# First layer's middle batches: the older batch's routing moved behind the fourth turn and the second product, and two weight steps moved to GpSimd

## Chip, cores and metric

One NeuronCore of a Trainium2 chip runs the whole kernel. The metric is the device time in microseconds of one execution. Engine names: PE is TensorE, DVE VectorE, ACT ScalarE, POOL GpSimd, SP SyncE.

## What is computed

Two rounds of gated cross-attention and feed-forward on `x` of shape (4, 512, 256), with a context of 64 rows. Cut to what the change touches:

```python
x = x + tanh(g_xattn[0]) * xattn0(layernorm(x), ctx)    # 16 heads, then relu(out @ W1 + b1) @ W2 + b2
x = x + tanh(g_ffn[0]) * moe(layernorm(x))              # router: logits = layernorm(x) @ router_w + router_b
x = x + tanh(g_xattn[1]) * xattn1(layernorm(x), ctx)
x = x + tanh(g_ffn[1]) * bitlinear_mlp(layernorm(x))    # weights rounded to -1, 0, 1 times mean(abs(w))
```

The change lies in the first line's stage. Beside the attention of the first layer, that stage does two side jobs: the router's logits of each finished batch (the second line's `layernorm(x) @ router_w`), and the rounding of the three weight matrices of the fourth line.

## The kernel before, in words

The order on each engine is written out by hand: each engine has its own program, an endless sequence of instructions in program order, and waits on semaphores. Nothing is reordered. The function `attention(l, b, first_batch, last_batch)` exists once for each of PE, ACT and DVE, and `batch(l, b, first, last)` is the same stretch on POOL. `l` is the layer, `b` the batch (0 to 3). Batches 1 and 2 of layer 0 are the middle batches.

A batch has four tiles of 128 rows (`i` = 0 to 3). The work of a tile:

- `scores` on PE writes s_tile[i % 2] in PSUM. DVE takes the maximum (`score_max`, L1515) and subtracts it into `probs` (`score_sub`, L1524), ACT takes the exponential (`exps`, L1163), DVE sums and inverts (`sums`, L1537 and L1540), POOL multiplies by the inverse (`normalise`, L523).
- `turn(i)` on PE transposes the tile (L761) into `t_bank`, and ACT copies it out (`turned`, L1201). `values(half)` on PE multiplies two tiles with the values (L779), ACT rounds the result to `o_hi` (L1206), DVE makes the rest `o_lo` (`lower_outputs`, L1608).
- At the end of a batch PE does the first product (L831, 36 matmuls) and the second product (L846, 48 matmuls). ACT makes `h_t` and `h_hi` between them, DVE `h_lo` (L1613). DVE adds the result to `x_res` (L1679), and takes its statistics (L1453, L1462).

Tiles 0 and 1 of batch b+1 are scored, summed and normalised within batch b. So a batch opens with `turn(0)`, `scores(b, 2)`, `turn(1)`, `scores(b, 3)` on PE.

The routing of the older batch b-1: POOL computes `rstd` (`layer_norm_rstd`, L407 and L409), DVE writes the normalised rows to `xn2` (`norm_apply`, L1475: four instructions of 128x256, shown as `ew<-x_res,mv,rstd` because `xn2` lies in the memory of `ew2`), SP stores them, PE transposes them (`router_turn`, L901), ACT copies them to `xn_t` (`router_rows`, L1168), PE multiplies (`router_products`, L908), DVE adds the bias (`router_logits`, L1581).

The weight rounding of matrix w has three elementwise steps on 128x2048: `ternary_first` (L1571) and `ternary_second` (L1577) on DVE, `ternary` (L489) on POOL. In the last batch PE transposes the results in six chunks (`ternary_chunk`, L894) and ACT copies them. Chunks 4 and 5 are of matrix 2.

The second use of L1475 (`xn<-x_res,mv,rstd`) is the normalisation of the rows for batch b+2, in batches 0 and 1.

## Time and profile before

| | |
|---|---|
| median of 3 runs | 578.87 us (573.36 to 580.24) |
| profiled execution, its own time | 582.83 us |
| its span | 580.0 us, so 2.8 us lie around it |
| mean granted TensorE clock | 0.933 |
| stage of the change, layer 0's four batches | 30.0 to about 166 us of the span |
| batch 1 (67.4 to 102.8): busy us of PE, DVE, ACT, POOL | 31.9, 32.4, 18.0, 15.2 of 35.4 |
| batch 2 (102.8 to 136.9): the same | 31.9, 28.2, 18.1, 14.9 of 34.1 |
| batch 3 (136.9 to 166.2): the same | 26.3, 17.6, 19.9, 9.3 of 29.3 |

The busy times say how full an engine is, and not which one is waited for. In this stage the engines hand tiles to each other every microsecond or two, so the chain of waits and the timeline are what to read. Times in the sections below are positions in this one execution.

### The profile page before, as it was taken

What the parts mean: (1) busy time and instruction counts of PE and PEld (TensorE: products, weight loads), DVE (VectorE), ACT (ScalarE), POOL (GpSimd) and SP (SyncE); (2) the same over time, 40 slices, a digit from 0 to 9 for tenths busy, and PEclk for the clock granted to TensorE, in tenths of its full rate; (3) what the DMA queues carried; (4) which work ended last, traced back from release to release, by engine and by line L of the source; (5) the groups of instructions that cost most, each with busy time, mean ns of one, the idle gap of its engine ahead of it and who ended that gap; (6) DMA issues with size and microseconds to landing.
All of it is one profiled execution on the core that took longest, in us unless ns stands there. A gap on an engine that the chain in (4) does not pass through costs nothing.

```text
span 580.0 us, 10094 instructions
## 1 busy us (share of the span) xinstructions
PE 493.1 (85%) x3060; PEld 358.4 (62%) x3068; DVE 408.4 (70%) x780; ACT 301.1 (52%) x537; POOL 244.7 (42%) x317
## 2 busy tenths in 40 slices
PE   8888898898997999799999999947578778568994
PEld 3445657576863578688888888823345545335652
DVE  6599999798466677494755833225988888588992
ACT  1355654565744356583755623302356564656884
POOL 5465263356100211020212110047267876638996
PEclk9989989899778599899999999979799999698999
DMA  7940000100636157635554310023000000000112
GB/s 211 307 150 1 17 21 1 38 1 0 201 100 208 28 165 246 203 134 172 184 179 153 99 31 23 18 65 90 0 1 0 2 2 0 1 0 2 36 36 72
DMA packets 35162, 46.40 MB, mean 80 GB/s; under 512 B 2764, under 2 KB 25304, under 8 KB 35128
## 3 DMA queue, kind: packets, MB, share of 16 engines
q1 hardware_dynamic: 30856, 39.02, 21.0%
q0 software_dynamic: 1680, 4.59, 2.8%
q10 hardware_dynamic: 2592, 2.36, 1.2%
q8 instruction: 18, 0.29, 0.2%
q14 instruction: 16, 0.13, 0.1%
HBM read 38.36 MB, written 7.60 MB: 79 GB/s over the span
## 4 chain that ended last, share of the span: by engine, by line
PE 47%; DVE 29%; POOL 7%; ACT 6%; issue 5%; DMA 2%; SPq 2%; DVEq 1%; POOLq 0%; ACTq 0%
PE s_tile L1002 17%; PE bank L1023 8%; DVE probs L1524 5%; DVE s_max L1515 5%; DVE p_sum L1537 5%; PE bank L846 4%; ACT probs L1163 3%; PE bank L1012 3%; DVE stats L1453 2%; PE s_tile L1096 2%; DMA w<-in_L_xattn_W 2%; PE bank L761 2%; DVE x_res L1679 1%; DVE ew L1577 1%; POOL xn_all L619 1%
## 5 line engine op out<-in xcount | busy, mean ns | idle before, releaser
L523 POOL TENSOR_TENSOR probs<-probs,p_rcp 128x1024 f32<-128x1024 f32 x32 | 63.8, 1994 | 77.7 <-DVE p_rcp L1540 77.7
L761 PE MATMUL bank<-ident,probs 128*128 128x128 f32 x256 | 39.4, 303 | 29.1 <-POOL probs L523 25.8
L1002 PE MATMUL s_tile<-ew_hi,xs_hi 128*128 128x512 f32 x144 | 59.9, 416 | 3.9 <-DVE ew_lo L1704 2.9
L1201 ACT COPY probs_t<-bank 128x512 f32<-128x512 f32 x64 | 34.9, 589 | 46.4 <-PE bank L761 46.3
L1002 PE MATMUL s_tile<-ew_hi,xs_lo 128*128 128x512 f32 x144 | 57.7, 401 | 0.0
L1002 PE MATMUL s_tile<-ew_lo,xs_hi 128*128 128x512 f32 x144 | 57.7, 400 | 0.0
L761 PEld LDWEIGHTS bank<-ident,probs 128*128 128x128 f32 x256 | 32.3, 156 | 40.9 <-POOL probs L523 29.8
L586 POOL TENSOR_TENSOR token_now<-token_of,carried 128x1 uint32<-128x1 uint32 x17 | 3.8, 222 | 127.0 <-PE bank L986 127.0
L1810 DVE TENSOR_TENSOR probs_t<-s_tile,probs_t 128x512 f32<-128x512 f32 x36 | 24.8, 689 | 43.5 <-PE s_tile L1002 42.0
L1163 ACT ACTIVATE probs<-probs 128x1024 f32<-128x1024 f32 x32 | 33.9, 1060 | 31.3 <-DVE probs L1524 31.2
L1537 DVE TENSOR_REDUCE p_sum<-probs 128x16 f32<-128x1024 f32 x32 | 38.8, 1214 | 13.2 <-ACT probs L1163 13.2
L1704 DVE TENSOR_TENSOR ew_lo<-ew,ew_hi 128x512 fp32r<-128x512 f32 x64 | 40.5, 685 | 10.5 <-ACT ew_hi L1287 10.3
L1515 DVE TENSOR_REDUCE s_max<-s_tile 128x16 f32<-128x1024 f32 x32 | 38.2, 1194 | 12.1 <-PE s_tile L745 12.1
L1023 PE MATMUL bank<-ew_hi,act_hi 128*128 x144 | 42.1, 292 | 0.0
L745 PE MATMUL s_tile<-k_bd,q_t 64*128 64x256 f32 x256 | 39.1, 420 | 2.7 <-ACT q_t L1158 2.7
L1287 ACT CAST ew_hi<-ew 128x512 fp32r<-128x512 f32 x64 | 35.5, 619 | 10.6 <-issue 7.3
L1023 PE MATMUL bank<-ew_hi,act_lo 128*128 x144 | 40.7, 283 | 0.0
L1023 PE MATMUL bank<-ew_lo,act_hi 128*128 x144 | 40.1, 279 | 0.0
L1524 DVE TENSOR_TENSOR probs<-s_tile,s_max 128x1024 f32<-128x1024 f32 x32 | 39.2, 1224 | 1.0
L1814 DVE TENSOR_TENSOR act_lo<-bank,act_hi 128x512 fp32r<-128x512 f32 x36 | 24.8, 689 | 18.7 <-ACT act_hi L1332 18.6
L1332 ACT CAST act_hi<-bank 128x512 fp32r<-128x512 f32 x36 | 21.2, 588 | 30.4 <-PE bank L1012 30.3
L1322 ACT ACTIVATE probs_t<-s_tile 128x512 f32<-128x512 f32 x36 | 21.6, 600 | 29.1 <-PE s_tile L1002 25.6
(244 smaller groups left out, 1301.5 us busy)
## 6 DMA issues: line engine op xcount, KB each, us to landing
ew<-in_L_ffn_w SPq DMA_DIRECT2D x32, 512.0 KB, 5.1
...
```

The lines of the kernel that those rows point to most:

```text
L523: nc.gpsimd.tensor_tensor(p, p, p_rcp[:, i, :].unsqueeze(2).to_broadcast([P, H, M]), ALU.mult).then_inc(s["p_norm"], 1)
L745: last = nc.tensor.matmul(s_bank[i % 2][g][:, GH * M * m:GH * M * m + GH * M], q_t[rows, m, P * i:P * i + P], flat(k_bd[rows, m, bass.ds(n ...
L761: last = nc.tensor.transpose(t_bank[c][:, P * j:P * j + P], probs[:, i % 2, at:at + P], ident[:])
L1002: last = nc.tensor.matmul(o[:], x, w, start=(k == 0 and n == 0), stop=(k == DK - 1 and n == 2))
L1023: last = nc.tensor.matmul(y_bank[:, D * par:D * par + D], u, w, start=(c == 0 and n == 0), stop=(c == EK - 1 and n == 2))
L1163: nc.scalar.activation(probs[:, i % 2, :], probs[:, i % 2, :], ACT.Exp).then_inc(att[l]["a_exp"], 1)
L1201: last = nc.scalar.copy(flat(probs_t[:, i % 2, 4 * c:4 * c + 4, :]), t_bank[c][:])
L1287: last = nc.scalar.copy(hi, w)
L1515: nc.vector.tensor_reduce(s_max[:, i, :], s_tile[i % 2][:].rearrange("p (h s) -> p h s", h=H), AX, ALU.max).then_inc(s["v_max"], 1)
L1524: nc.vector.tensor_tensor(probs[:, i % 2, :].rearrange("p (h s) -> p h s", h=H), s_tile[i % 2][:].rearrange("p (h s) -> p h s", h=H), s_ma ...
L1537: nc.vector.tensor_reduce(p_sum[:, i, :], probs[:, i % 2, :].rearrange("p (h s) -> p h s", h=H), AX, ALU.add).then_inc(s["v_sum"], 1)
L1704: last = nc.vector.tensor_tensor(lo, w, hi.bitcast(F32), ALU.subtract)
```

## The change

On DVE, the two rounding steps go. They become `ternary_steps` on POOL, one batch later, at the start of `batch`. `norm_apply` of the older rows moves from the start of the batch (or the end of the one before) to behind `sums(l, b, 3)`. `router_logits` moves to the end of the batch.

On PE, `router_turn` moves from behind `scores(b, 3)` to behind `turn(3)`, into `s_bank[1]`. `router_products` moves from the middle of `values(0)` to behind the second product, into `older_logits`, which lies in s_tile 0. The scores of tile 1 of the next batch move whole behind `values(1)`. The scores of tile 2 get a wait for `r_lg`, the signal of DVE's `router_logits`.

On ACT, in middle batches, the rows of the next batch and the first output are copied ahead of the exponential of tile 2, and `router_rows` moves behind `turned(3)`.

On POOL, `bias_rows` of the last batch moves from its start to behind `normalise(3)`, and `ternary` moves behind `normalise(3)` in middle batches and behind `normalise(2)` in the last.

```diff
@@ -483,9 +483,17 @@
 
                 nc.gpsimd.tensor_tensor(carried[:, 3 + use:4 + use], carried[:, 2:3], carried[:, 2:3], ALU.add)
 
+            def ternary_steps(w):
+
+                raw = bit_raw[:, w, :]
+                pool.wait_ge(v_tern, w + 1)
+                nc.gpsimd.tensor_scalar(raw, raw, w_inv[:, w:w + 1], 1.0, ALU.mult, ALU.min).then_inc(p_terq, 1)
+                pool.wait_ge(p_terq, 3 * w + 1)
+                nc.gpsimd.tensor_scalar(raw, raw, -1.0, ROUND, ALU.max, ALU.add).then_inc(p_terq, 1)
+
             def ternary(w):
 
-                pool.wait_ge(v_tern, 3 * w + 3)
+                pool.wait_ge(p_terq, 3 * w + 2)
                 nc.gpsimd.tensor_scalar(bit_q[:, w, :], bit_raw[:, w, :], -ROUND, 1.0, ALU.add,
                                         ALU.mult).then_inc(p_terq, 1)
 
@@ -537,18 +545,22 @@
                                         ALU.mult).then_inc(ln["l1"]["xn"], 1)
 
             def batch(l, b, first, last):
-                if last:
+                if l == 0 and not first:
+                    ternary_steps(b - 1)
+                if l == 1 and last:
                     bias_rows(l, b)
+                normalise(l, b, 2)
                 if l == 0 and last:
                     ternary(b - 1)
-                normalise(l, b, 2)
                 if l == 0 and first:
                     lower_second_weights()
-                if l == 0 and not (first or last):
-                    ternary(b - 1)
                 if l == 1 and not last:
                     bias_rows(l, b)
                 normalise(l, b, 3)
+                if l == 0 and last:
+                    bias_rows(l, b)
+                if l == 0 and not (first or last):
+                    ternary(b - 1)
                 if b + 2 < B:
                     layer_norm_rstd(pool, ln["l0" if l == 0 else "l1"], b + 3)
                 if l == 1 and not first:
@@ -723,8 +735,6 @@
                 for m in range(DK):
                     if l == 0 and m == 1 and not start:
                         pe.wait_ge(v_wm, n)
-                        if not first:
-                            pe.wait_ge(r_lg, n - 1)
                     if not start:
                         left = v_olo if l == 0 else s["a_o"]
                         pe.wait_ge(left, 2 * DK * n - 2 * DK + m + 1)
@@ -739,6 +749,8 @@
                     pe.wait_ge(s["a_q"], DK * n + DK)
                 if i >= 2 and 0 in chunks:
                     pe.wait_ge(s["v_sub"], TB * n + i - 1)
+                if l == 0 and i == 2 and n >= 2:
+                    pe.wait_ge(r_lg, n - 1)
                 for m in chunks:
                     for g in range(G):
                         rows = slice(GP * g, GP * g + GP)
@@ -782,8 +794,6 @@
 
                 def between():
 
-                    if l == 0 and not (first_batch or last_batch):
-                        router_products(b - 1, logit_out)
                     if l == 0 and not last_batch:
                         weight_sum(b)
                     if not last_batch:
@@ -794,8 +804,6 @@
                 turn(1)
                 scores(l, b, 3)
                 pe.wait_ge(s["a_pt"], TB * b + 2)
-                if l == 0 and not (first_batch or last_batch):
-                    router_turn(b - 1, t_bank)
                 values(0)
                 if not last_batch:
                     queries(l, b + 1, first_batch, False)
@@ -809,15 +817,17 @@
                 if not last_batch:
                     scores(l, b + 1, 0)
                 turn(3)
-                if l == 0 and last_batch:
-                    pe.wait_ge(s["v_sub"], TB * b + TB)
+                pe.wait_ge(s["v_sub"], TB * b + TB)
+                if l == 0 and not first_batch:
                     router_turn(b - 1, s_bank[1])
-                if not last_batch:
-                    pe.wait_ge(s["v_sub"], TB * b + TB)
+                elif not last_batch:
                     scores(l, b + 1, 1, (0,))
                 values(1)
-                if l == 0 and not last_batch:
+                if l == 0 and first_batch:
                     scores(l, b + 1, 1, (1,))
+                elif l == 0 and not last_batch:
+                    pe.wait_ge(r_e, DK * b)
+                    scores(l, b + 1, 1)
                 if l == 1 and not first_batch:
                     ff_turn(b - 1)
                 if l == 0:
@@ -868,6 +878,9 @@
                             last = nc.tensor.matmul(att_bank[1][i][:, 0:D], o_t[:, k, P * i:P * i + P], wo[:, k, :],
                                                     start=(k == 0), stop=(k == DK - 1))
                         last.then_inc(s["t_y"], 1)
+                if l == 0 and not (first_batch or last_batch):
+                    pe.wait_ge(s["v_sub"], TB * b + TB + 2)
+                    router_products(b - 1, older_logits)
                 if not (l == 0 and last_batch):
                     pe.wait_ge(s["v_y"], TB * b + 2)
 
@@ -881,7 +894,7 @@
 
                 w, c = n // 2, n % 2
                 if c == 0:
-                    pe.wait_ge(p_terq, w + 1)
+                    pe.wait_ge(p_terq, 3 * w + 3)
                 if n == 0:
                     pe.wait_ge(att[0]["v_sub"], NT - 1)
                 if n >= 2:
@@ -1218,13 +1231,14 @@
                 turned(0)
                 turned(1)
                 if l == 0 and not (first_batch or last_batch):
-                    router_rows(b - 1, t_bank)
-                exps(l, b, 2)
-                output(0, 0)
-                if not last_batch:
-                    if l == 0 and not first_batch:
-                        act.wait_ge(r_l, b)
+                    output(0, 0)
                     turned_rows(l, b + 1)
+                    exps(l, b, 2)
+                else:
+                    exps(l, b, 2)
+                    output(0, 0)
+                    if not last_batch:
+                        turned_rows(l, b + 1)
                 output(0, 1)
                 if l == 1 and not first_batch:
                     ff_norm(b - 1)
@@ -1245,6 +1259,8 @@
                 if l == 0 and last_batch:
                     ternary_chunk(5)
                 turned(3)
+                if l == 0 and not (first_batch or last_batch):
+                    router_rows(b - 1, s_bank[1])
                 if l == 1 and not last_batch:
                     exps(l, b + 1, 0)
                 output(1, 0)
@@ -1561,21 +1577,6 @@
                 dve.wait_ge(v_wm, w + 1)
                 nc.vector.reciprocal(w_inv[:, bass.ds(w, 1)], w_mean[:, bass.ds(w, 1)]).then_inc(v_tern, 1)
 
-            def raw_weights(w):
-                return bit_raw[:, bass.ds(w, 1), :].rearrange("p o a -> p (o a)")
-
-            def ternary_first(w):
-
-                raw = raw_weights(w)
-                dve.wait_ge(v_tern, 3 * w + 1)
-                nc.vector.tensor_scalar(raw, raw, w_inv[:, bass.ds(w, 1)], 1.0, ALU.mult, ALU.min).then_inc(v_tern, 1)
-
-            def ternary_second(w):
-
-                raw = raw_weights(w)
-                dve.wait_ge(v_tern, 3 * w + 2)
-                nc.vector.tensor_scalar(raw, raw, -1.0, ROUND, ALU.max, ALU.add).then_inc(v_tern, 1)
-
             def router_logits(b, src):
                 dve.wait_ge(r_l, b + 1)
                 nc.vector.tensor_tensor(logits[:, bass.ds(b * TB, TB), :],
@@ -1613,9 +1614,10 @@
                     nc.vector.tensor_tensor(h1_lo[:, m, :], h1_t[:, m, :], h1_hi[:, m, :].bitcast(F32),
                                             ALU.subtract).then_inc(v_hlo, 1)
 
-                if l == 0 and not (first_batch or last_batch):
+                if l == 0 and not first_batch:
                     score_sub(l, b, 2)
-                    scores(l, b, 3)
+                    if not last_batch:
+                        scores(l, b, 3)
                 else:
                     scores(l, b, 2)
                 if last_batch:
@@ -1636,15 +1638,15 @@
                     lower_outputs(0, 1)
                     weight_scale(b)
                 if l == 0 and not (first_batch or last_batch):
-                    router_logits(b - 1, logit_out)
+                    sums(l, b, 3)
+                    if b > 1:
+                        dve.wait_ge(d_rows, 16 * b - 16)
+                    norm_apply(second, b, TB * b - TB, xn2)
                 if ahead:
 
                     row_stats(phase, TB * b + 2 * TB)
-                if not (l == 0 and last_batch):
+                if l == 1 or first_batch:
                     sums(l, b, 3)
-                if l == 0 and not last_batch:
-                    ternary_first(b)
-                    ternary_second(b)
                 if l == 1 and not first_batch:
                     dve.wait_ge(second["rstd"], 2 * b - 1)
                 if ahead:
@@ -1689,11 +1691,12 @@
                     join_stats(second, b + 1)
                 else:
                     norm_stats(second, b + 1, TB * b)
-                if l == 0 and b != B - 2:
-                    if not last_batch:
-                        score_max(l, b + 1, 2)
-                    if not first_batch:
-                        dve.wait_ge(d_rows, 16 * b)
+                if l == 0 and not (first_batch or last_batch):
+                    router_logits(b - 1, older_logits)
+                if l == 0 and not last_batch:
+                    score_max(l, b + 1, 2)
+                if l == 0 and last_batch:
+                    dve.wait_ge(d_rows, 16 * b)
                     norm_apply(second, b + 1, TB * b, xn2)
 
             for b in range(B):
```

POOL, from the end of batch 1 to the first tiles of batch 3. Here L523 is `normalise`, L407 and L409 are `rstd`, L478 is `bias_rows`, L489 the third rounding step. Before:

```order
L523 TENSOR_TENSOR probs<-probs,p_rcp 128x1024 [waits v_rcp_l0]
L489 TENSOR_SCALAR ew<-ew 128x2048 [waits v_tern]
L523 TENSOR_TENSOR probs<-probs,p_rcp 128x1024 [waits v_rcp_l0]
L478 TENSOR_TENSOR x_res<-x_res,bo 128x1024 [waits ln_xn_l0]
L523 TENSOR_TENSOR probs<-probs,p_rcp 128x1024 [waits v_rcp_l0] x2
L407 TENSOR_TENSOR var_eps<-mv,eps 128x4 [waits ln_aggr_rt]
L409 TENSOR_TENSOR rstd<-var_eps,minus_half 128x4 [waits ln_eps_rt]
L478 TENSOR_TENSOR x_res<-x_res,bo 128x1024 [waits ln_xn_l0]
L489 TENSOR_SCALAR ew<-ew 128x2048 [waits v_tern]
L523 TENSOR_TENSOR probs<-probs,p_rcp 128x1024 [waits v_rcp_l0] x2
```

And in the changed kernel, where L531 is `normalise`, L490 and L492 are the moved rounding steps and L497 the third:

```order
L490 TENSOR_SCALAR ew<-ew,w_inv 128x2048 [waits v_tern]
L492 TENSOR_SCALAR ew<-ew 128x2048 [waits p_terq]
L531 TENSOR_TENSOR probs<-probs,p_rcp 128x1024 [waits v_rcp_l0] x2
L497 TENSOR_SCALAR ew<-ew 128x2048 [waits p_terq]
L478 TENSOR_TENSOR x_res<-x_res,bo 128x1024 [waits ln_xn_l0]
L531 TENSOR_TENSOR probs<-probs,p_rcp 128x1024 [waits v_rcp_l0] x2
L407 TENSOR_TENSOR var_eps<-mv,eps 128x4 [waits ln_aggr_rt]
L409 TENSOR_TENSOR rstd<-var_eps,minus_half 128x4 [waits ln_eps_rt]
L490 TENSOR_SCALAR ew<-ew,w_inv 128x2048 [waits v_tern]
L492 TENSOR_SCALAR ew<-ew 128x2048 [waits p_terq]
L531 TENSOR_TENSOR probs<-probs,p_rcp 128x1024 [waits v_rcp_l0]
L497 TENSOR_SCALAR ew<-ew 128x2048 [waits p_terq]
```

In batch 2, `normalise(2)` and `normalise(3)` stood around one rounding step. Now two steps stand ahead of them, and a third step and the bias stand right behind `normalise(3)`, with no wait that holds them back. In batch 3 the third step stands between the two `normalise`.

DVE, from the end of batch 1 through the middle of batch 2. Before:

```order
L1537 TENSOR_REDUCE p_sum<-probs 128x16 [waits a_exp_l0]
L1540 RECIPROCAL p_rcp<-p_sum 128x16 [waits v_sum_l0]
L1608 TENSOR_TENSOR o_lo<-bank,o_hi 128x256 [waits a_o_l0] x2
L1559 TENSOR_SCALAR w_mean<-bank 128x1 [waits t_abs]
L1562 RECIPROCAL w_inv<-w_mean 128x1 [waits v_wm]
L1581 TENSOR_TENSOR logits<-bank,rb 128x32 [waits r_l]
L1537 TENSOR_REDUCE p_sum<-probs 128x16 [waits a_exp_l0]
L1540 RECIPROCAL p_rcp<-p_sum 128x16 [waits v_sum_l0]
L1571 TENSOR_SCALAR ew<-ew,w_inv 128x2048 [waits v_tern]
L1577 TENSOR_SCALAR ew<-ew 128x2048 [waits v_tern]
L1515 TENSOR_REDUCE s_max<-s_tile 128x16 [waits t_s_l0]
```

And in the changed kernel, where L1491 is `norm_apply`, L1582 `router_logits`, L1531 and L1540 the maximum and the subtraction:

```order
L1553 TENSOR_REDUCE p_sum<-probs 128x16 [waits a_exp_l0]
L1556 RECIPROCAL p_rcp<-p_sum 128x16 [waits v_sum_l0]
L1609 TENSOR_TENSOR o_lo<-bank,o_hi 128x256 [waits a_o_l0] x2
L1575 TENSOR_SCALAR w_mean<-bank 128x1 [waits t_abs]
L1578 RECIPROCAL w_inv<-w_mean 128x1 [waits v_wm]
L1553 TENSOR_REDUCE p_sum<-probs 128x16 [waits a_exp_l0]
L1556 RECIPROCAL p_rcp<-p_sum 128x16 [waits v_sum_l0]
L1491 TENSOR_SCALAR ew<-x_res,mv,rstd 128x256 [waits ln_rstd_rt,ln_aggr_rt,d_rows]
L1491 TENSOR_SCALAR ew<-x_res,mv,rstd 128x256 x3
L1531 TENSOR_REDUCE s_max<-s_tile 128x16 [waits t_s_l0]
```

`norm_apply` stood between the maximum and the subtraction of tile 2. It now stands behind the sums of tile 3, where the two rounding steps were. The adding of the logits stands behind the statistics, ahead of the maximum.

PE, the opening of batch 2. Before, with L901 as `router_turn`:

```order
L761 MATMUL bank<-ident,probs 128x128 [waits p_norm_l0,v_y_l0]
L761 MATMUL bank<-ident,probs 128x128 x7
L745 MATMUL s_tile<-k_bd,q_t 128x256 [waits v_sub_l0]
L745 MATMUL s_tile<-k_bd,q_t 128x256 x3
L761 MATMUL bank<-ident,probs 128x128 [waits a_pt_l0,p_norm_l0]
L761 MATMUL bank<-ident,probs 128x128 x7
L745 MATMUL s_tile<-k_bd,q_t 128x256 [waits v_sub_l0]
L745 MATMUL s_tile<-k_bd,q_t 128x256 x3
L901 MATMUL bank<-ident,ew 128x128 [waits ln_xn_rt,a_pt_l0]
L901 MATMUL bank<-ident,ew 128x128 x7
```

And in the changed kernel, from the last row of the end of batch 1, with L921 as `router_products`:

```order
L921 MATMUL s_tile<-rw,xn_t 128x8 [waits r_e,v_sub_l0]
L921 MATMUL s_tile<-rw,xn_t 128x8 x7
L773 MATMUL bank<-ident,probs 128x128 [waits p_norm_l0,v_y_l0]
L773 MATMUL bank<-ident,probs 128x128 x7
L757 MATMUL s_tile<-k_bd,q_t 128x256 [waits r_lg,v_sub_l0]
L757 MATMUL s_tile<-k_bd,q_t 128x256 x3
L773 MATMUL bank<-ident,probs 128x128 [waits a_pt_l0,p_norm_l0]
L773 MATMUL bank<-ident,probs 128x128 x7
L757 MATMUL s_tile<-k_bd,q_t 128x256 [waits v_sub_l0]
L757 MATMUL s_tile<-k_bd,q_t 128x256 x3
```

The products now stand ahead of the first turn, and the scores of tile 2 wait for `r_lg`. The two router rows between the scores and the values are gone.

## Rows read from the trace of the kernel before

**Rows 1.** The chain of waits, batches 1 and 2: start, length in us, what.

```profile
77.69 1.31 DVE stats L1453 x4
...
93.30 5.67 PE bank L846 x45
...
117.26 2.81 DVE ew L1577
```

**Rows 2.** The timeline, batch 1: start, length in us, engine, line, instruction, idle before.

```profile
69.29 1.38 DVE L1475 TENSOR_SCALAR ew<-x_res,mv,rstd 128x256 f32<-128x256 f32 x4 [0.38 <-POOL rstd L409]
...
74.11 1.21 DVE L1537 TENSOR_REDUCE p_sum<-probs 128x16 f32<-128x1024 f32 x1
...
75.31 1.07 ACT L1153 COPY xn_t<-bank 128x512 f32<-128x512 f32 x2 [1.54 <-PE bank L717]
...
75.69 1.91 POOL L523 TENSOR_TENSOR probs<-probs,p_rcp 128x1024 f32<-128x1024 f32 x1 [6.51 <-DVE p_rcp L1540]
...
76.91 0.42 DVE L1608 TENSOR_TENSOR o_lo<-bank,o_hi 128x256 fp32r<-128x256 f32 x1 [1.02 <-ACT o_hi L1206]
...
80.32 1.20 DVE L1571 TENSOR_SCALAR ew<-ew,w_inv 128x2048 f32<-128x2048 f32 x1
...
80.49 2.79 POOL L523 TENSOR_TENSOR probs<-probs,p_rcp 128x1024 f32<-128x1024 f32 x1 [1.03 <-DVE p_rcp L1540]
...
81.55 2.81 DVE L1577 TENSOR_SCALAR ew<-ew 128x2048 f32<-128x2048 f32 x1
...
84.63 1.19 DVE L1515 TENSOR_REDUCE s_max<-s_tile 128x16 f32<-128x1024 f32 x1
```

**Rows 3.** The timeline, batch 2, VectorE and GpSimd.

```profile
109.63 1.21 DVE L1537 TENSOR_REDUCE p_sum<-probs 128x16 f32<-128x1024 f32 x1
...
118.95 3.34 POOL L478 TENSOR_TENSOR x_res<-x_res,bo 128x1024 f32<-128x1024 f32 x1
...
119.99 1.21 DVE L1515 TENSOR_REDUCE s_max<-s_tile 128x16 f32<-128x1024 f32 x1
```

**Rows 4.** The timeline, the first normalisation beside the key spreading.

```profile
11.45 0.71 POOL L458 TENSOR_TENSOR k_bd<-k_t,group_mask 128x256 f32<-128x256 f32 x1 [0.28 <-ACT k_t L1144]
...
11.61 0.70 DVE L1475 TENSOR_SCALAR xn<-x_res,mv,rstd 128x256 f32<-128x256 f32 x1
...
12.13 0.66 POOL L458 TENSOR_TENSOR k_bd<-k_t,group_mask 128x256 f32<-128x256 f32 x1
```

**Rows 5.** The timeline, the end of batch 1.

```profile
96.84 2.91 DVE L1475 TENSOR_SCALAR xn<-x_res,mv,rstd 128x256 f32<-128x256 f32 x4
...
99.67 1.65 DVE L1679 SCALAR_TENSOR_TENSOR x_res<-bank,tg,x_res 128x256 f32<-128x256 f32 x4
...
100.59 1.09 PE L761 MATMUL bank<-ident,probs 128*128 128x128 f32 x8 [1.27 <-DVE x_res L1679]
...
103.21 1.19 DVE L1515 TENSOR_REDUCE s_max<-s_tile 128x16 f32<-128x1024 f32 x1
```

**Rows 6.** The timeline, router products of batch 1, end of batch 2.

```profile
72.61 1.95 PE L908 MATMUL bank<-rw,xn_t 128*128 128x8 f32 x16 [0.16 <-ACT xn_t L1168]
...
133.74 0.48 DVE L1679 SCALAR_TENSOR_TENSOR x_res<-bank,tg,x_res 128x256 f32<-128x256 f32 x1 [1.25 <-PE bank L846]
...
134.67 1.09 PE L761 MATMUL bank<-ident,probs 128*128 128x128 f32 x8
```

**Rows 7.** The timeline, batch 3.

```profile
141.07 1.90 POOL L489 TENSOR_SCALAR ew<-ew 128x2048 bf16<-128x2048 f32 x1
...
145.20 1.01 PE L894 MATMUL s_tile<-ident_b,ew 128*128 128x128 bf16 x8 [1.33 <-ACT up_t L1173]
...
145.61 2.91 DVE L1475 TENSOR_SCALAR ew<-x_res,mv,rstd 128x256 f32<-128x256 f32 x4
...
150.41 1.36 PE L901 MATMUL s_tile<-ident,ew 128*128 128x128 f32 x8
```

**Rows 8.** Busy time by stretch, batch 1: stretch, length, engines, clock, DMA.

```profile
76.00:80.00 4.00, 4.00 (x13) 1.67 (x6) 3.05 (x9) 1.81 (x4) 3.46 (x2) 0.58 0.00 0
```

## The prediction

> **What bounds the kernel now.** The change touches layer 0 only, 136 of the 580 us of the span, and the rest should follow it unchanged. I read the chain of waits first, to see which engine ends the waits in this stage: it goes back and forth between DVE and PE, and both moved jobs stand on it. The second rounding step L1577 is in it for 2.81 us in every batch that has one, and so are the statistics and the second product [rows 1]. The timeline then tells why L1577 takes so long. Its twin L1571 of the same size takes 1.20; L1577 takes 2.81 because POOL's `normalise` lies beside it, and that takes 2.79 where the same instruction took 1.91 without such a neighbour [rows 2]. So these two kinds of instruction exclude each other: DVE's L1571, L1577 and L1475 on one side, anything on POOL on the other. Who gets in next is to be seen at the start of the kernel, where eight short POOL instructions stand in a row beside a `norm_apply` of four: each DVE instruction after the first takes 0.70 instead of about 0.35, having waited for one POOL instruction, and POOL's take turns with them [rows 4]. They alternate, instruction by instruction. Where POOL has one instruction only, `norm_apply` takes 2.91 instead of 1.38 [rows 2, 5].
>
> This is what decides the change. It frees DVE of two rounding steps. It also puts `norm_apply` at the moment at which POOL starts `normalise(3)`, with more POOL work queued behind it.
>
> **Batch 0.** Rounding off DVE lets POOL's third `normalise` take 1.9 instead of 2.8, as the pair in batch 1 shows [rows 2]. `turn(3)` waits for it. Gain 0.9. The exponential and the copies that follow are unchanged. Sum -0.9.
>
> **Batch 1, first half.** `norm_apply` goes from between the maximum and the subtraction: 1.38 and the 0.38 of waiting for `rstd` [rows 2], 1.7 in all. Some of it comes back, since ACT now makes two copies (1.07) ahead of the exponential that DVE's sums wait for [rows 2]. I take 0.5 given back; the bounds are 0 (`router_turn` no longer stands ahead of the copies on PE) and 1.07. The sums start at 74.1 - 0.9 - 1.2 = 72.0. On POOL, the two moved steps start with the batch. L489 has their size and takes 1.90 [rows 7], so I take 3.8 together; the bounds are 2.4 (DVE's 1.20 each) and 5.6 (L1577's 2.81 each) [rows 2]. POOL stood idle for 6.51 before `normalise(2)` [rows 2], so they cost nothing here. If that cover were gone, they would cost all of it.
>
> **Batch 1, second half.** Before, the DVE ran from the sums at 74.11 to L1571 at 80.32 [rows 2], 6.2 us. Of this, 1.0 was a wait for `o_hi` that should go (PE has less ahead of it), and 1.3 were statistics, which now stand behind `norm_apply` [rows 1, 2]. That leaves 3.9, so `norm_apply` starts at 75.9, when POOL starts `normalise(3)`. Its first instruction goes through. The second waits for `normalise(3)` (1.9), the third for the third rounding step (1.9), which is queued right behind. The fourth is free. So 1.4 + 3.3 (of each POOL instruction some 0.2 is cover by DVE's own time) = 4.7, to 80.6. Statistics and their joining add 1.7: the next maximum starts at 82.3, and before at 84.63 [rows 2]. DVE leads by 2.3. To the end of the batch DVE stays ahead by that much: `x_res` at 99.67 - 2.3 = 97.4 [rows 5]. But PE now ends its second product at 93.30 - 2.3 + 5.7 = 96.7 and then makes the router products. They took 72.61 to 74.4, 1.8 us [rows 6]. So `turn(0)` starts at 98.5, and before at 100.59 [rows 5]. Lead 2.1.
>
> **Batch 2.** Here the new wait for `r_lg` bites. The scores of tile 2 can only start when DVE has added the logits, behind `x_res` and its statistics. Behind these scores PE's whole queue stands, `turn(1)` first. From the start of `x_res` to the maximum it took 3.54 [rows 5]. So the logits are there at 97.4 + 3.6 = 101.0, the scores take 1.1 with 0.2 for the signals, and the maximum starts at 102.3, and before at 103.21. Lead 0.9. `norm_apply` goes again (1.2 net), so the sums start at 109.63 - 2.1 = 107.5 [rows 3], and `norm_apply` 3.9 later at 111.4. This time POOL has three instructions in its queue: `normalise(3)` 1.9, rounding 1.9 and `bias_rows`. The last showed 3.34, of which it waited until 120.07, where L1577 ended, so its own work is 2.2 [rows 1, 3]. Each of the last three instructions of `norm_apply` waits for one of them. It ends at 111.4 + 6.0 + 1.0 = 118.4, instead of 112.8. The maximum of the next batch starts at 118.5, and before at 119.99 [rows 3]: lead 1.5. `router_turn` stands behind the same `norm_apply`, so PE gets no further ahead either. The second product ends 1.5 earlier. Batch 2 has no `norm_apply` at its end, so PE was ahead there: DVE waited 1.25 for it [rows 6]. The router products now cost their full 1.8, and `turn(0)` of batch 3 starts at 134.67 - 1.5 + 1.8 = 135.0 [rows 6]. The lead is gone, -0.3 to +0.3.
>
> **Batch 3.** The wait for `r_lg` costs nothing more: logits at 133.74 - 1.5 + 3.6 = 135.8, scores to 137.0, about where DVE's maximum stood. On POOL the third rounding step of matrix 2 comes behind `normalise(2)`. It ended at 143.0 [rows 7]. Now it has to wait for `normalise(2)`, which ends about when DVE reaches its `norm_apply`, 145.5, since the inverse of tile 2 is ready one sum and a maximum's length earlier. So the step ends at 147.4. Chunk 4 on PE, at 145.20 before [rows 7], waits for it: +2.3 there. DVE's `norm_apply` at 145.61 took 2.91 with one POOL neighbour [rows 7]. Now it has the rest of the rounding step, `normalise(3)`, and `bias_rows`, moved behind it: to 152.2 instead of 148.5. `router_turn` started at 150.41 [rows 7]. Now it starts at 152.3, +1.9. The first product waits for the values behind it. I take +1.5 at the end of the batch, since PE's own transposes there ran long before and can catch up some 0.4.
>
> **Sum.** 0.0 + 1.5 = +1.5 us, of the profiled execution's 582.83: 584.3. That execution lies 4 us above the median of the runs, 578.87. The difference carries over: 578.87 + 1.5 = 580.4. A measurement of this kernel can hardly tell less than 2% from no change, 11.6 us. The three runs alone lie 6.9 apart. So I forecast no change, with a small loss.
>
> **A rule of the Trainium skill.** The rows show DVE and POOL taking turns by whole instructions [rows 4], and the sum rests on it. The Trainium skill, page "SBUF — State Buffer", section "SBUF: two separate sides", says that the port pair that the two engines share is an exclusive lock, held for the whole instruction, for which the other one fully blocks. By that rule, the trace agrees, and it speaks against this change, which adds POOL instructions beside `norm_apply`. A split of bandwidth instead of a lock would give the time of the first rival.
>
> **Rivals.**
> First, the stall comes once per `norm_apply` and not two or three times. The 2.91 rows show one each [rows 5, 7], and there POOL had nothing queued behind. If DVE's four instructions kept the turn once they had it again, batch 1 would gain 1.6 more, batch 2 4.0, batch 3 2.0. Of these 7.6, the PE path lets some 5 through, since values and products bind next: 580.4 - 5 = 575.4. Against it speaks the alternation of rows 4.
> Second, slower: PE's clock. Between 76 and 80 the granted clock was 0.58 of full, so mostly 1.2 GHz [rows 8], after a stretch in which PE had waited and had done the narrow router products. The change makes PE wait between `turn(0)` and `scores(2)` right behind those same products, in batches 2 and 3. If the clock falls there, scores, `turn(1)` and scores take twice their 3.2 us, with DVE waiting for each. Half of the 3.2 is hidden by DVE's maximum and subtraction, so 1.6 in batch 2 and 1.6 in batch 3: 580.4 + 3.2 = 583.6, 0.8% slower than before. It decides from the point at which both falls lie within the first 4 us of a batch. For it speaks that idle; against it, that the queries at 76.4 then run at full clock, though DVE hides that gain.
> Third, the wait for `r_lg` does not bind, because the logits arrive before PE asks. It needs DVE 2.4 us earlier than I have it. It saves the 1.3 by which the maximum of batch 2 then starts earlier: 579.1. This is within the forecast.
> Fourth, the change does not do what it says: `norm_apply` slips in ahead of `normalise(3)` whole and DVE keeps its full relief of 4 us in each of three batches, less the products' 1.8 in two. 578.87 - 12 + 3.6 = 570.5. The queue order makes it unlikely: both wait for the same `rcp`.
>
> **How the numbers follow.** Forecast 0.45 (578.5 to 582), first rival 0.2, second 0.2, third 0.1, fourth 0.05. The range takes in the first and second rival and half of the runs' own spread of 6.9 on either side: 572 to 586. Faster by over 2% means below 567.3 and needs more than the fourth rival: 0.03. Slower by over 2% means above 590.4: 0.02. Within 2%: 0.95.
>
> **What would show it.** In the changed profile, `norm_apply` to `ew` should take about 4.7, 7 and 6.6 us in batches 1, 2 and 3, split by POOL's instructions. With 2.9 each, the first rival holds. Between `turn(0)` and the scores of tile 2, PE should idle some 1.3 us in batch 2 and less in batch 3, with DVE's logits as the releaser. `turn(0)` should start at 64.2, 98.5 and 135.0, chunk 4 near 147.5, and the rounding steps on POOL should be near 1.9 each. What would make me wrong is another alternation than in rows 4, or a clock that falls in other places.

## The result: 3.9% slower, and the profile after

| | |
|---|---|
| kernel before, median | 578.81 us (573.36 to 580.24, 4 runs) |
| changed kernel, median | 600.72 us (599.37 to 603.23, 4 runs) |
| ratio | 1.039, 95% interval 1.0349 to 1.043 |
| profiled execution: span, own time, mean granted clock | 601.0, 603.23, 0.925 |
| forecast | 580.4 (572 to 586), no change |

Times count every execution; the ratios here and below leave out those that were over 1.5% longer than the fastest of the same kernel.

The forecast was wrong by 20 us: it said no change, and the kernel is 3.9% slower. The timeline of POOL after the change tells at once where the time goes. It shows start, length in us, engine, line, instruction, and in brackets the idle time before. L490 and L492 are the two moved steps, L497 is the third step (L489 before), L531 is `normalise`.

```profile
67.29 7.17 POOL L490 TENSOR_SCALAR ew<-ew,w_inv 128x2048 f32<-128x2048 f32 x1
74.55 7.10 POOL L492 TENSOR_SCALAR ew<-ew 128x2048 f32<-128x2048 f32 x1
81.63 3.82 POOL L531 TENSOR_TENSOR probs<-probs,p_rcp 128x1024 f32<-128x1024 f32 x2
85.43 1.93 POOL L497 TENSOR_SCALAR ew<-ew 128x2048 bf16<-128x2048 f32 x1
...
109.47 7.16 POOL L490 TENSOR_SCALAR ew<-ew,w_inv 128x2048 f32<-128x2048 f32 x1
116.72 7.09 POOL L492 TENSOR_SCALAR ew<-ew 128x2048 f32<-128x2048 f32 x1
```

Three instructions over the same 2048 elements: 7.17, 7.10 and 1.93. The two steps take 14.3 us per matrix, where the forecast had 3.8. POOL's idle time ahead of the third `normalise`, 6.51 before [rows 2], is gone, and that `normalise` now starts at 81.63 and not at 75.69.

The timeline of DVE and PE shows who pays. L1491 is `norm_apply` (L1475 before), L1681 the addition to `x_res`, L773 `turn`, L907 `ternary_chunk`.

```profile
70.94 1.22 DVE L1553 TENSOR_REDUCE p_sum<-probs 128x16 f32<-128x1024 f32 x1 [0.26 <-ACT probs L1176]
...
74.64 12.87 DVE L1491 TENSOR_SCALAR ew<-x_res,mv,rstd 128x256 f32<-128x256 f32 x4
...
104.48 1.65 DVE L1681 SCALAR_TENSOR_TENSOR x_res<-bank,tg,x_res 128x256 f32<-128x256 f32 x4
...
120.34 9.31 DVE L1491 TENSOR_SCALAR ew<-x_res,mv,rstd 128x256 f32<-128x256 f32 x4
...
143.68 1.66 DVE L1681 SCALAR_TENSOR_TENSOR x_res<-bank,tg,x_res 128x256 f32<-128x256 f32 x4 [0.82 <-PE bank L856]
```

```profile
63.22 1.09 PE L773 MATMUL bank<-ident,probs 128*128 128x128 f32 x8 [1.70 <-DVE x_res L1681]
...
83.60 1.97 PE L773 MATMUL bank<-ident,probs 128*128 128x128 f32 x8 [7.06 <-POOL probs L531]
...
166.89 1.03 PE L907 MATMUL s_tile<-ident_b,ew 128*128 128x128 bf16 x8 [11.57 <-POOL ew L497]
```

There are two victims. In batch 1 `norm_apply` takes 12.87 us for four instructions of 0.35. The view of the tile gives shortest, median and longest of the four in ns:

```profile
L1491 DVE TENSOR_SCALAR ew<-x_res,mv,rstd x4: 1978/1982/7160, 74.6 to 85.5; 128x256 f32<-128x256 f32 x4
```

The longest started 0.09 behind L492 and waited for all of it. The other three took 1.98 each, one for each `normalise` and one for L497. The other victim is PE: it waits 7.06 for the third `normalise` in batch 1, and 11.57 for the last rounding step in batch 3. The start of `x_res` is a good clock for the stage. It stood at 99.67 [rows 5], 133.74 [rows 6] and, in batch 3 of the same timeline, at 163.55. Now it stands at 104.48, 143.68 and 184.25: +4.8, +9.9, +20.7. Batch 3 before, and then after:

```profile
163.55 0.48 DVE L1679 SCALAR_TENSOR_TENSOR x_res<-bank,tg,x_res 128x256 f32<-128x256 f32 x1 [2.62 <-PE bank L846]
```

```profile
184.25 0.48 DVE L1681 SCALAR_TENSOR_TENSOR x_res<-bank,tg,x_res 128x256 f32<-128x256 f32 x1 [2.62 <-PE bank L856]
```

The span grew by 21.0, so all but 0.3 of the loss lies in layer 0.

The chain of waits (start, length, what) now runs over both steps, in batches 1 and 3:

```profile
67.30 7.18 POOL ew L490
74.55 7.10 POOL ew L492
81.65 1.91 POOL probs L531
83.60 1.97 PE bank L773 x8
...
155.95 7.09 POOL ew L492
163.03 1.90 POOL probs L531
164.93 1.92 POOL ew L497
166.89 1.03 PE s_tile L907 x8
```

### The profile page after: what moved, and what is told of

Its sections match the earlier page's. It is cut to its first block, busy times and chain, and to the rows that moved or that the text cites. A ratio compares the mean times of both kernels' runs of the same rounds, so it can differ in the third digit from the quotient of the medians.

```text
span 601.0 us, 10106 instructions
## 1 busy us (share of the span) xinstructions
PE 494.6 (82%) x3067; PEld 360.8 (60%) x3068; DVE 425.9 (71%) x774; ACT 301.7 (50%) x537; POOL 281.8 (47%) x323
## 4 chain that ended last, share of the span: by engine, by line
PE 51%; DVE 25%; POOL 11%; ACT 7%; issue 5%; DVEq 1%; DMA 0%; POOLq 0%; ACTq 0%
PE s_tile L1015 16%; PE bank L1036 8%; DVE p_sum L1553 4%; DVE s_max L1531 3%; DVE probs L1540 3%; PE bank L1025 3%; PE s_tile L1109 3%; PE bank L841 3%; POOL ew L490 2%; PE bank L773 2%; POOL ew L492 2%; PE s_tile L757 2%; ACT probs L1176 2%; DVE stats L1469 2%; PE bank L742 2%
## 5 line engine op out<-in xcount | busy, mean ns | idle before, releaser
L531 POOL TENSOR_TENSOR probs<-probs,p_rcp 128x1024 f32<-128x1024 f32 x32 | 61.1, 1912 | 64.2 <-DVE p_rcp L1556 64.2
L773 PE MATMUL bank<-ident,probs 128*128 128x128 f32 x256 | 40.9, 311 | 34.8 <-POOL probs L531 30.6
L773 PEld LDWEIGHTS bank<-ident,probs 128*128 128x128 f32 x256 | 33.2, 161 | 47.5 <-POOL probs L531 38.2
L1531 DVE TENSOR_REDUCE s_max<-s_tile 128x16 f32<-128x1024 f32 x32 | 38.3, 1197 | 16.8 <-PE s_tile L757 16.7
L757 PE MATMUL s_tile<-k_bd,q_t 64*128 64x256 f32 x256 | 40.4, 435 | 4.5 <-ACT q_t L1171 2.4
L742 PE MATMUL bank<-xn_t,wq 128*128 128x512 f32 x64 | 31.5, 634 | 10.7 <-DVE o_lo L1609 6.1
L1540 DVE TENSOR_TENSOR probs<-s_tile,s_max 128x1024 f32<-128x1024 f32 x32 | 39.2, 1225 | 1.1
```

The source lines that it names most:

```text
L531: nc.gpsimd.tensor_tensor(p, p, p_rcp[:, i, :].unsqueeze(2).to_broadcast([P, H, M]), ALU.mult).then_inc(s["p_norm"], 1)
L742: last = nc.tensor.matmul(x_bank[m][:], wq[l][:, k, m * P:m * P + P], xn_t[:, k, :], start=(k == 0), stop=(k == DK - 1))
L757: last = nc.tensor.matmul(s_bank[i % 2][g][:, GH * M * m:GH * M * m + GH * M], q_t[rows, m, P * i:P * i + P], flat(k_bd[rows, m, bass.ds(n ...
L773: last = nc.tensor.transpose(t_bank[c][:, P * j:P * j + P], probs[:, i % 2, at:at + P], ident[:])
L1531: nc.vector.tensor_reduce(s_max[:, i, :], s_tile[i % 2][:].rearrange("p (h s) -> p h s", h=H), AX, ALU.max).then_inc(s["v_max"], 1)
L1540: nc.vector.tensor_tensor(probs[:, i % 2, :].rearrange("p (h s) -> p h s", h=H), s_tile[i % 2][:].rearrange("p (h s) -> p h s", h=H), s_ma ...
```

## Experiments

Times are medians, or of one execution where that is said, and each ratio is against the kernel before on the same chip, with its 95% interval.

**1. Are min and max the expensive thing?** The clamps are left out:

```diff
-tensor_scalar(raw, raw, w_inv[:, w:w + 1], 1.0, ALU.mult, ALU.min)
-tensor_scalar(raw, raw, -1.0, ROUND, ALU.max, ALU.add)
+tensor_scalar(raw, raw, w_inv[:, w:w + 1], 1.0, ALU.mult, ALU.mult)
+tensor_scalar(raw, raw, 0.0, ROUND, ALU.add, ALU.add)
```

> The changed kernel with both clamps left out of the steps on POOL: multiply, multiply and add, add in place of multiply, min and max, add (so the weights are rounded but not held to -1, 0, 1). Theory: min and max are what costs 7.1 us on POOL. Then both steps take about 1.9 us, norm_apply 4.7 to 7, and the time is that of my sum, 580.4 (578 to 584). Rival A: the per-row scale or the writing in place costs, not the operation. Then the steps stay at 7.1 and the time at about 600. Rival B: the moved routing costs most of the 22 us. Then the steps are short and the time still above 590.

587.91 us, 1.012 (1.0074 to 1.0167). The first step fell to 1.99, but the second, add with add and no clamp in it, stayed at 7.10. So my theory was wrong as I had put it: it is not min and max as such.

**2. Which forms are short?** Three kernels, each profiled once, with other forms in the same two places.

> One look at six forms of the same instruction on POOL, 128x2048 f32 in place (the weights are not quantised as they should be). Matrix 0: per-row scale with multiply and multiply; then max alone. Matrix 1: multiply by a constant and min; then add and add. Matrix 2: max and min in one; then the per-row scale with multiply alone. Theory (clamps cost): 1.9, 7.1, 7.1, 1.9, 7.1 or more, 1.9. If a clamp has a price of its own of 5.2 us, max with min takes 12.4; if any clamp sends the whole instruction down a slow path, it takes 7.1. Rival (the per-row scale costs): 7.1 in the two forms that have it, 1.9 in the others. Time about 596 to 604 either way.

> One look at six more forms on POOL, 128x2048 f32 in place (the weights are not quantised as they should be). The first look gave 1.9 to 2.0 for multiply with multiply and for add with multiply, 7.1 for add with add, multiply with min, max with min and max with add, and 5.4 for one operation alone (max, or the multiply by the per-row scale). Matrix 0: per-row scale with multiply and add; then multiply and subtract by constants. Matrix 1: max and multiply; then multiply and max. Matrix 2: subtract and multiply; then add and add with constants other than zero. Theory: only pairs with a multiply and no min or max are fast: 2.0, 2.0, 7.1, 7.1, 2.0, 7.1. Rival: only the literal pairs add, multiply and multiply, add and multiply, multiply are fast: then those with subtract take 7.1.

> One look at six more forms on POOL, f32 in place (the weights are not quantised as they should be). Matrix 0, 2048 elements: multiply and add by constants; then add and multiply with f32 out. Matrix 1, 2048 elements: multiply alone; then min alone. Matrix 2, 1024 elements: max and min; then multiply and add. Theory: only the three pairs multiply-multiply, multiply-add and add-multiply are short: 2.0, 1.9, 5.4, 5.4, 3.6, 1.0, the slow ones by the element. Rival: a single multiply by a constant is short, and 5.4 was the price of the per-row scale: 1.9.

One row each of a short pair (multiply, add), of a slow pair (add, add) and of a single operation (multiply alone):

```profile
66.92 1.99 POOL L492 TENSOR_SCALAR ew<-ew,w_inv 128x2048 f32<-128x2048 f32 x1
```

```profile
150.05 7.11 POOL L496 TENSOR_SCALAR ew<-ew 128x2048 f32<-128x2048 f32 x1
```

```profile
101.52 5.40 POOL L492 TENSOR_SCALAR ew<-ew 128x2048 f32<-128x2048 f32 x1
```

The table at the end lists all forms. Of the theories written down, "clamps cost" fell with add, add (7.11) and the lone multiply (5.45), for both of which it had 1.9. "A multiply and no min or max" fell with multiply, subtract (7.12) and subtract, multiply (7.11). "Only the pairs multiply-multiply, multiply-add and add-multiply are short" met all its six numbers in the third kernel. One operation alone is slower (5.4) than a short pair. The per-row scale costs at most 0.1 (1.99 against 1.90), and the writing in place nothing that shows.

**3. The two halves of the change.** The routing alone (rounding back on DVE), and the rounding alone (old routing, `ternary_steps` at the head of the batch on POOL):

```diff
 # routing alone, DVE, behind sums(l, b, 3)
+                if l == 0 and not last_batch:
+                    ternary_first(b)
+                    ternary_second(b)
```

> The routing part alone: the changed kernel's PE, ACT and DVE order, with the rounding steps back on DVE behind the third sums, and POOL's order as before. Theory: the routing part is not what costs; norm_apply is split by one or two of POOL's instructions, the router's products cost 1.8 in two batches, and the time is 579 to 586. Rival B: the moved routing costs most of it, then 592 or more.

> The rounding part alone: the kernel before with the two rounding steps on POOL at the head of each batch and POOL's order as in the changed kernel. Theory: 14.3 us on POOL per matrix, of which the 6.5 idle ahead of the third normalise hide a part; turn(2) and whatever DVE instruction needs the shared side wait for the rest, some 6 to 8 us in each of three batches: 594 to 603. Rival B: 577 to 583.

| | median | ratio |
|---|---|---|
| routing alone | 585.83 | 1.0122 (1.004 to 1.0204) |
| rounding alone | 626.52 | 1.0798 (1.0734 to 1.0863) |
| both, the change | 600.72 | 1.039 (1.0349 to 1.043) |

I had expected 594 to 603 of the rounding alone. It cost 46 us. In the old routing `norm_apply` stands between a maximum and its subtraction, where POOL begins its 14.3 us:

```profile
67.50 15.03 DVE L1487 TENSOR_SCALAR ew<-x_res,mv,rstd 128x256 f32<-128x256 f32 x4 [0.37 <-POOL rstd L409]
82.45 1.21 DVE L1536 TENSOR_TENSOR probs<-s_tile,s_max 128x1024 f32<-128x1024 f32 x1
```

One DVE instruction waits for L490, one for L492, and everything waits for them. So the halves are not additive: the new routing, slower by itself, saved more than half of what the rounding cost, by getting `norm_apply` out of that place.

**4. Does the place matter?** The same two slow steps, the first one moved to where POOL stood idle ahead of the next batch's second `normalise`.

```diff
-                    ternary_steps(b - 1)      # head of the batch
+                    ternary_second(b - 1)     # head of the batch
...
+                    ternary_first(b)          # ahead of normalise(l, b + 1, 1)
```

> The changed kernel, with the first of its two rounding steps on POOL moved to where POOL idled 4.7 to 6.2 us (ahead of the next batch's second normalise), the second at the head of the batch. Same instructions, same 14.3 us per matrix. Theory: what costs is what sticks out of POOL's idle time and locks out norm_apply. Now 2.4 stick out at the first place (7.2 less 4.8), and the second step ends at about the time at which the third normalise is due: 588 to 594. Rival: POOL's own work counts wherever it stands: 600.

602.91, 1.0438 (1.0395 to 1.0482): the rival's number, and not to be told from the change's own 1.039 (1.0349 to 1.043), but not for the rival's reason. Batch 1 of this run:

```profile
92.77 7.17 POOL L490 TENSOR_SCALAR ew<-ew,w_inv 128x2048 f32<-128x2048 f32 x1
93.06 6.64 DVE L1620 TENSOR_TENSOR h_lo<-h_t,h_hi 128x512 fp32r<-128x512 f32 x4
...
98.55 0.58 PE L862 MATMUL bank<-w_hi,h_hi 128*128 128x256 f32 x1 [5.16 <-DVE h_lo L1620]
```

POOL was idle there, but DVE makes `h_lo` at that moment, for which the second product waits. Four `h_lo` of 0.68 take 6.64, and PE waits 5.16. The first of the four was held for 4.84; the other three then took 0.68 each, while L490 still ran. I had counted POOL's idle time and not what DVE does beside it. So `h_lo` is one more instruction that POOL locks out, though not for the whole of L490.

**5. What is left with two short steps?** The changed kernel with pairs that are both short (clamps left out):

```diff
+tensor_scalar(raw, raw, w_inv[:, w:w + 1], 1.0, ALU.mult, ALU.mult)
+tensor_scalar(raw, raw, 1.0, ROUND, ALU.mult, ALU.add)
```

> The changed kernel with both steps in pairs that were short: the per-row scale with multiply and multiply, then multiply and add (the clamps are left out, so the weights are rounded but not held to -1, 0, 1). Everything else as in the changed kernel. Theory: the miss lies in the length of the two steps alone; with 1.9 to 2.0 each the x_res of batch 3, 163.55 before and 184.25 after the change, starts at about 165 (the forecast's +1.5), norm_apply takes 4.4 to 4.8, 6 to 7 and 6 to 6.6 in batches 1, 2 and 3, and the time is 580 to 586, where the routing alone gave 585.8. Rival: even short steps on POOL cost by their locking (norm_apply in particular): x_res of batch 3 at 168 or later, 588 or more.

587.53, 1.0176 (1.0101 to 1.0251). The steps took 1.99 and 1.92. `norm_apply` and what PE waited for, in batches 1, 2 and 3:

```profile
76.49 4.45 DVE L1491 TENSOR_SCALAR ew<-x_res,mv,rstd 128x256 f32<-128x256 f32 x4
...
114.36 6.54 DVE L1491 TENSOR_SCALAR ew<-x_res,mv,rstd 128x256 f32<-128x256 f32 x4
...
148.31 6.51 DVE L1491 TENSOR_SCALAR ew<-x_res,mv,rstd 128x256 f32<-128x256 f32 x4
```

```profile
137.44 1.07 PE L773 MATMUL bank<-ident,probs 128*128 128x128 f32 x8
...
150.14 1.03 PE L907 MATMUL s_tile<-ident_b,ew 128*128 128x128 bf16 x8 [3.57 <-POOL ew L497]
```

`x_res` of batch 3 starts at 167.78: +4.2 against 163.55, where the change had +20.7.

```profile
167.78 0.48 DVE L1681 SCALAR_TENSOR_TENSOR x_res<-bank,tg,x_res 128x256 f32<-128x256 f32 x1 [2.60 <-PE bank L856]
```

So 16.5 of the 20.7 us are the length of two instructions. The median lies between theory and rival, and `x_res` at 167.78 is all but the rival's 168: the short steps and the routing together still cost something.

**6. What the routing costs.** Logits ahead of the statistics, and POOL's last step away from `norm_apply`, each on the routing alone:

> The routing part alone again, with DVE adding the router's logits between x_res and the statistics, not behind them. In the routing run DVE's maximum of tile 2 waited 1.32 us for PE's scores in batches 2 and 3, and PE 1.04 for the logits. Theory: that wait is worth about 2.6 of the 5 us that the routing part cost; with the logits 1.8 earlier it goes: 582 to 584. Rival: the wait hides another limit of the same length, then 585 to 586.

> The routing part alone again, with POOL's last rounding step in batches 1 and 2 moved from between the normalises of tiles 2 and 3 to ahead of the next batch's second normalise, away from norm_apply. Theory: norm_apply pays for one POOL instruction less, 1.9 us: it goes from 4.35 to about 2.9 in batch 1 and from 6.39 to about 4.5 in batch 2; of these 3.4 the path gets at most what PE lets through: 582 to 585. Rival: POOL's queue moves up and norm_apply meets bias_rows in its place: no change in its length, 585 to 586.

581.47, 1.0105 (1.0027 to 1.0183), and 584.84, 1.0156 (1.0101 to 1.021). With intervals of a percent, neither can be told from the routing alone (1.0122). In the second one `norm_apply` fell from 4.35 and 6.39 to 2.88 and 4.95, as expected. `x_res` of batch 3 came at 163.94 and not at 164.73, so of these 2.9 only 0.8 reached the end of the stage. The step had moved beside `h_lo`: four of them took 3.94 in batches 1 and 2 and not 2.63, and PE waited 1.73 and 2.12 for them and not 1.04 and 1.01. It is experiment 4 again.

**7. Round first, then clamp.** Clamping after rounding gives the same values, and puts a short pair on POOL and one instruction of 1.2 us on DVE:

```diff
+nc.gpsimd.tensor_scalar(raw, raw, w_inv[:, w:w + 1], ROUND, ALU.mult, ALU.add)
+nc.vector.tensor_scalar(raw, raw, ROUND - 1.0, ROUND + 1.0, ALU.max, ALU.min)
```

> The kernel before, with other rounding steps and nothing else moved. POOL multiplies by the scale and adds the rounding constant (multiply, add) ahead of the next batch's second normalise, where it stood idle for 4.7 to 5.5 us; DVE holds the result between the constant less one and the constant plus one in a single instruction (max, min) ahead of x_res; POOL's last step stays. Theory: the pair multiply, add is one of the fast ones and takes about 2.0, hidden by that idle time; DVE has 1.2 per batch in place of 1.2 and 2.8, so up to 2.8 come back in each of three batches, less what PE holds back: 572 to 577. Rival: PE ends the waits there anyway, then 579 to 582. If the pair is slow (7.1), the second normalise is 2 to 3 late in each batch: 583 to 588.

> The same rounding steps in the changed kernel's routing, with POOL's order as before. Theory: the routing part alone cost 5 us (its run gave 1.012 of before), since norm_apply then stands beside two or three of POOL's instructions; with these rounding steps DVE gets 2.8 back per batch as above, and the time is 577 to 582. Rival: the routing was slow only because of the two DVE steps behind norm_apply; then as fast as the same steps in the old routing, or faster: 576 or less.

> The changed kernel's routing with everything that should help it: round first (multiply and add on POOL, one clamp on DVE), logits ahead of the statistics, POOL's last step late. Theory: 585.0 (the run with round first) less 2.6 for the wait and 1 to 2 for norm_apply: 580 to 582, no better than the kernel before, because the router's products then cost PE their 1.85 in batches where DVE does not hide them. Rival: 577 or less; then this routing is good and only its company was bad.

> The kernel before with round first, placed by what its last run showed: there DVE's maximum waited 2.47 and 2.91 us for PE's scores in batches 1 and 2 where the two DVE steps had been, and the clamp stood 1.2 us on DVE's path at the end of the batch. Now POOL rounds ahead of the fourth normalise, DVE clamps behind the third sums, in that wait, and POOL's last step stands ahead of the next batch's second normalise. Theory: the 1.1 us gained per batch stays and the clamp costs nothing: 2 to 4 less than before, 575 to 577. Rival: PE's limit moves with it, within 1 of before.

| | routing | median | ratio |
|---|---|---|---|
| round first | old | 581.71 | 1.0044 (1.0014 to 1.0074) |
| round first | new | 584.96 | 1.0122 (1.008 to 1.0163) |
| the same, logits first, last step late | new | 584.04 | 1.0123 (1.0066 to 1.0179) |
| round first, clamp in DVE's wait for PE | old | 583.87 | 1.0111 (1.0064 to 1.0158) |

The pair took 1.98 to 2.00 (2.95 twice in the third kernel, beside `h_lo`), near the forecast's 2.0, but no time came back. In the last one the maximum of the next batch came at 82.36, and before at 84.63 [rows 2]; 1.1 of this lead stem from batch 0, whose `x_res` started at 63.06 and not at 64.19. Yet `x_res` came at 99.52, and before at 99.67 [rows 5]. Between these, POOL and DVE of the last kernel:

```profile
91.09 1.90 POOL L495 TENSOR_SCALAR ew<-ew 128x2048 bf16<-128x2048 f32 x1
```

```profile
91.39 3.95 DVE L1613 TENSOR_TENSOR h_lo<-h_t,h_hi 128x512 fp32r<-128x512 f32 x4
```

It is experiment 4 on a small scale. POOL's last step, put into the same idle time, locks out `h_lo`: PE waits 1.53 for it, and the second product starts at 94.18, where before it started at 93.30 [rows 1].

```profile
94.18 0.38 PE L852 MATMUL bank<-w_hi,h_hi 128*128 128x256 f32 x1 [1.53 <-DVE h_lo L1613]
```

The other three kernels of this table have it too: each puts a step on POOL into that idle time, and their four `h_lo` of batch 1 take 4.04, 4.05 and 5.66.

**8. The last step clear of `h_lo`.** One edit of the kernel above:

```diff
                 if l == 0 and not last:
                     bias_rows(l, b)
+                    ternary(b)
                 if not last:
                     normalise(l, b + 1, 0)
-                    if l == 0:
-                        ternary(b)
                     normalise(l, b + 1, 1)
```

> The last kernel (round first, placed in the batch) with one edit: POOL's last step stands right behind bias_rows, beside DVE instructions on PSUM and reductions, and no longer beside h_lo. Theory: h_lo was locked out by it, and the second product starts 1 to 1.5 us earlier in batches 0 to 2; 574 to 578, and x_res of batch 3 at 160 to 162. Rival: PE's own work sets the end of the batch; then the second product starts as before the edit, 94.2, and the time is 582 to 585.

571.43 us, 0.987 (0.9815 to 0.9925): the one version that is faster than the kernel before, by 1.3%, so within the forecast's 2%. POOL and DVE of its batch 1:

```profile
85.43 1.89 POOL L495 TENSOR_SCALAR ew<-ew 128x2048 bf16<-128x2048 f32 x1
```

```profile
90.02 1.28 DVE L1612 TENSOR_TENSOR h_lo<-h_t,h_hi 128x512 fp32r<-128x512 f32 x2
```

PE no longer waits for `h_lo`: the 1.53 in each of batches 1 and 2 are gone. The second product starts at 91.36 and not at 94.18, and `x_res` of batch 3 at 160.61 and not at 164.55. Between the medians lie 12 us, but they can't be put down to `h_lo`. Of the 3.9 us in layer 0, the profiles show 1.5 behind the `h_lo` of batch 2. Another 1.4 were there in batch 1 before its `h_lo` began: in the kernel without the edit PE ran at a granted clock of 0.70 from 72 to 76, and here at 1.00. The rest, 1.0, came in batch 3, where neither kernel has a step on POOL beside `h_lo`, and where the clock was 0.50 from 148 to 152 without the edit and 1.00 with it.

The larger part lies behind layer 0, in instructions that the edit doesn't touch. They took 420.3 us without the edit (584.9 less 164.55) and 410.6 with it, and here too the clock differs, most of all from 190 to 200. Without the edit, then with it (length, PE busy, clock, DMA):

```profile
190.00:200.00 10.00, 9.08 (x27) 0.50 0.09 26
```

```profile
190.00:200.00 10.00, 7.76 (x37) 1.00 0.44 134
```

The kernel before has such executions too: 572.63 and 572.84 on this chip, at a mean clock of 0.955, where the five fastest of this version took 569.8 to 573.9 at 0.956 to 0.959. The mean clock of all its runs is 0.952, against 0.936 without the edit. Whether the shorter layer 0 brings the higher clock, or these runs were lucky in it, is not shown.

**9. How much a single profile says.** The kernel before twice more, and the routing alone once more, one profiled execution each:

> The kernel before, unchanged, one more look. Theory: the first profile of before had a fall of the clock in batch 3 (0.5 from 144 to 150) that its usual runs don't have; without it the x_res of batch 3 starts 2 to 3 us earlier, at 161 to 162, and the span is 575 to 577. Rival: x_res is at 163.5 again, and the spread of the spans lies behind layer 0.

> The kernel before, unchanged, a third look, for the spread between executions. Same two cases: 161 to 162 or 163.5 for the x_res of batch 3.

> The routing part alone, one more look on the same chip. Theory: x_res of batch 3 at 164.7 as in its first look, since no fall of the clock lay in its layer 0; span 580 to 586. Rival: it varies by as much as before does, and the 1.2 us between the first two looks say nothing.

`x_res` of batch 3 came at 162.71 and 162.84 in the two new profiles of before (163.55 in the first), and at 167.49 in the new one of the routing alone (164.73 in the first). So before varies by 0.8 and the routing alone by 2.8, and the routing is later in every pair, by 1.2 to 4.8. My guess about the clock in batch 3 fell: it was at 0.50 from 144 to 150 in both new profiles of before too, and the spans were 580.1 and 580.0 again. The routing alone had no such fall in its first profile (1.00 from 144 to 156) and had one in its second (0.53 from 148 to 152, 0.61 from 152 to 156), and 1.9 of its 2.8 arose in that batch.

## Why the prediction was wrong

**The step that failed** is the one in "Batch 1, first half": "L489 has their size and takes 1.90, so I take 3.8 together; the bounds are 2.4 and 5.6". Measured: 7.17 + 7.10 = 14.3. I took the price from an instruction with the same size and the same name, but with other operations, add and multiply where the moved ones have multiply, min and max, add. All bounds were of that kind or DVE's own. No row of before had POOL at any such pair, so an upper bound was missing, and the range was built on a term that had none. The experiments give this term 16.5 of the 20.7 us in layer 0. The Trainium skill, page "GPSIMD Engine Reference", section "Engine selection", puts add, multiply and max in one row and calls one-input elementwise work roughly line-rate on GpSimd. For the pairs with min or max (7.08 to 7.17, where the clamping step took 1.20 on DVE [rows 2]) and for add with add (7.10) the rows here speak against it.

**"If that cover were gone, they would cost all of it."** This sentence held. With 14.3 against an idle time of 6.51 the cover was gone, and the rest stood before `normalise(2)` and inside `norm_apply`.

**The alternation** was right. Forecast 4.7, 7.0 and 6.6 for `norm_apply`, and with short steps it took 4.45, 6.54 and 6.51. The first rival (one stall each, 575.4) and the fourth (`norm_apply` slips in whole) are out. In the changed kernel it took 12.87, 9.31 and 11.82, by the same mechanism with a longer neighbour. The whole-instruction lock that the Trainium skill, page "SBUF — State Buffer", section "SBUF: two separate sides", states is borne out by the 7.16 beside L492's 7.10, and not by the `h_lo` beside L490, which was held for 4.84 of 7.17.

**`sums(2)` at 72.0 and `turn(0)` at 64.2** came at 70.94 and 63.22, so the first half of batch 1 went 1 us better than forecast. The gain stems from batch 0, and is no more than the spread: in the three profiles of before, `x_res` of batch 0 starts at 64.19, 64.88 and 63.53.

**`r_lg`**: forecast a wait of PE of 1.3 in batch 2 and less in batch 3. With short steps PE waited 1.83 and 0.26, and DVE's maximum behind it 2.26 and 1.32. The rival in which the wait does not bind is out.

**"To the end of the batch DVE stays ahead by that much"** did not hold. With short steps the next maximum of batch 1 came at 82.65, near the forecast's 82.3 and 2.0 ahead of before, but `x_res` at 98.69 was 1.0 ahead (99.67 before), where I had 2.3.

**Batch 3, +1.5**: the batch was sized right, its start was not. With short steps `x_res` of batch 2 came at 134.92, where I had 132.2 (133.74 less 1.5). From there to `x_res` of batch 3 it took 32.9, against 29.8 before. That is 3.1 more, and the forecast had 3.0, from a lead of 1.5 to a loss of 1.5. Chunk 4 at 150.14 instead of 147.5, after a wait of 3.57 for POOL, and `turn(0)` at 137.44 instead of 135.0 are late by that start. So even with short steps layer 0 is 4.2 longer, not 1.5, and the difference arose in batches 1 and 2.

**The clock (second rival)**: it fell in the changed kernel behind the long waits. `turn(2)` at 83.60 took 1.97 and not 1.04, and from 110 to 112 the granted clock was 0.51, the lower of the two levels. With short steps it fell where the rival has it, in batch 2: 0.54 from 102 to 104, and the scores of tile 2 took 2.08 and not the 1.14 of batch 3, where it did not fall. As sized, 3.2 us, it could never have explained 20.

**"The difference carries over"** from the profiled execution to the median: not settled. The short-step kernel shows +4.2 in layer 0 and +1.8% in its runs, some 10 us. The routing alone shows +1.2 and +4.8 in two profiles and 1.2%, some 7 us. In the profiled executions nothing is lost behind layer 0: from `x_res` of batch 3 to the end of the span it took 416.0 with short steps, 417.4 and 417.3 with the routing alone, 416.8 in the changed kernel, and 416.5, 417.4 and 417.2 before. But all three profiles of before are of its slower executions (582.4 to 582.8, the median being 578.8), so against them the loss comes out too small. The mean granted clock of the runs is 0.930 and 0.938, against 0.942 and 0.943 of before on the same chips, so a part may be PE's clock. That is argued and not shown.
